# The last 69 adjacency visits inside the first aggregation, and a reordered context stretch

## Time and profile before

| | |
|---|---|
| time of the profiled execution | 481.68 us |
| its span, first to last instruction | 479.9 us |
| granted TensorE clock, mean | 0.992 |
| PE busy | 456.2 us (95%), 2517 matmuls |
| VectorE busy | 327.6 us (68%) |
| ScalarE, GpSimd busy | 154.1 us (32%), 66.2 us (14%) |
| 262 of the visits on TensorE (L749) | 35.9 us |
| their marks on VectorE (L1850, L1851) | 68.1 and 64.6 us |

### The profile page before, as it was taken

The page is one execution under the profiler, slowest core; times in us unless marked ns, Lnnn a source line. Parts: engine busy times, 40 slices in busy tenths (PEclk is TensorE's granted clock), DMA queues, the critical chain, the costliest instruction groups (busy, mean ns, idle before and its releaser), DMA issues.

```text
span 479.9 us, 7046 instructions
## 1 busy us (share of the span) xinstructions
PE 456.2 (95%) x2517; PEld 365.4 (76%) x2517; DVE 327.6 (68%) x1108; ACT 154.1 (32%) x282; POOL 66.2 (14%) x95
## 2 busy tenths in 40 slices
PE   8999996899999999989999999999999998978996
PEld 5777785678778786968887999987877775655784
DVE  6988597668887978789997011244655656778982
ACT  4665882204223142342123111121223123660110
POOL 5434600000000000000000400000500000006662
PEclk9999998989999999999999999999999999999999
DMA  8910200170000000020300000000754439604892
GB/s 266 264 48 2 88 0 1 19 197 21 2 1 0 2 0 2 2 87 2 122 2 0 5 0 1 1 1 0 259 156 133 136 121 325 221 2 140 283 378 80
DMA packets 20415, 40.46 MB, mean 84 GB/s; under 512 B 2521, under 2 KB 2851, under 8 KB 20373
## 3 DMA queue, kind: packets, MB, share of 16 engines
q1 hardware_dynamic: 18117, 32.53, 21.6%
q0 software_dynamic: 2256, 7.39, 4.4%
HBM read 30.09 MB, written 10.31 MB: 84 GB/s over the span
## 4 chain that ended last, share of the span: by engine, by line
PE 71%; DVE 20%; ACT 4%; issue 3%; DMA 1%; POOLq 0%; POOL 0%; SPq 0%; DVEq 0%
PE ps L762 27%; PE ps L1104 9%; PE ps L1026 9%; PE ps L945 6%; PE ps L749 4%; PE ps L963 3%; DVE RING_D L1850 2%; DVE RING_S L1851 2%; PE ps L804 2%; ACT scrap_a L1529 1%; PE ps L890 1%; DVE QTL L1783 1%; DVE ESUM L1770 1%; PE ps L1121 1%; ACT QTH L1259 1%
## 5 line engine op out<-in xcount | busy, mean ns | idle before, releaser
L1850 DVE TENSOR_SCALAR RING_D<-places,PLACES 125x170 bf16<-125x170 f16 (+1 forms) x262 | 68.1, 260 | 0.0
L1851 DVE TENSOR_SCALAR RING_S<-iota,HOME 125x128 bf16<-125x128 f16 x262 | 64.6, 246 | 0.0
L749 PE MATMUL ps<-RING_D,RING_S 125*125 125x170 bf16 (+1 forms) x262 | 35.9, 246 | 2.7
L1026 PE MATMUL ps<-AT,H1H 125*128 125x416 f32 (+1 forms) x108 | 38.0, 352 | 0.1
L1026 PE MATMUL ps<-AT,H1L 125*128 125x416 f32 (+1 forms) x108 | 38.0, 351 | 0.0
L749 PEld LDWEIGHTS ps<-RING_D,RING_S 125*125 125x125 bf16 x262 | 26.6, 136 | 14.6 <-DVE RING_S L1851 7.5
L1104 PE MATMUL ps<-H2H,AT 125*125 125x512 f32 x90 | 36.1, 402 | 0.0
L1121 PE MATMUL ps<-WE0H 128*128 128x512 f32 x129 | 35.5, 408 | 0.0
L1104 PE MATMUL ps<-H2L,AT 125*125 125x512 f32 x90 | 35.5, 394 | 0.0
L623 POOL TENSOR_TENSOR G2L<-RAW_G,G2H 128x512 fp32r<-128x512 f32 x4 | 5.0, 1292 | 205.5 <-ACT G2H L1259 205.5
L1998 DVE SCALAR_TENSOR_TENSOR ZL<-ps,ZH 128x416 fp32r<-128x416 f32 (+1 forms) x12 | 6.3, 585 | 39.1 <-ACT ZH L1471 39.1
(11 more groups left out here) (416 smaller groups left out, 1174.6 us busy)
## 6 DMA issues: line engine op xcount, KB each, us to landing
RAW_E<-in_experts SPq DMA_DIRECT2D x8, 1024.0 KB, 10.1
RAW_AGAIN<-in_experts SPq DMA_DIRECT2D x3, 1024.0 KB, 11.8
X<-in_x SPq DMA_DIRECT2D x1, 2240.0 KB
out_x<-X SPq DMA_DIRECT2D x10, 224.0 KB
scratch<-X SPq DMA_DIRECT2D x10, 224.0 KB
scratch<-Y SPq DMA_DIRECT2D x10, 224.0 KB
RAW<-in_mW2T SPq DMA_DIRECT2D x4, 256.0 KB, 4.2
RAW_A<-in_mW SPq DMA_DIRECT2D x4, 256.0 KB, 4.6
```

The lines of the kernel that those rows point to most:

```text
L749: pe.matmul(PS[4 + g % 2][0:TT, o:o + width(b)], hot_s(v)[:, 0:TT], hot_d(v, width(b)), start=(s == 0), stop=(s == VISITS[b] - 1), skip_gr ...
L1026: pe.matmul(place(f), h[0:TT, k, 128 * f:128 * (f + 1)], AT[0:TT, k, c0:c1], start=(k == 0 and n == 0), stop=False)
L1850: V.tensor_scalar(hot_d(v, width(b)), places[0:ET, 0:width(b)], PLACES[0:ET, c:c + 1], None, ALU.is_equal)
L1851: V.tensor_scalar(hot_s(v), iota[0:ET, :], HOME[0:ET, c:c + 1], None, ALU.is_equal).then_inc(done["marked"], 1)
```

## The change

- `Z_BANKS` gives the aggregation's units their banks: chunk 0 on 2, 3, 0, 1, chunk 1 on 6, 7, 2, 3, chunk 2 on 0, 1, 4, 5; before these were 0 to 3, 4 to 7, 0 to 3.
- `visits_in_products` has 69 visits fewer in the products before the aggregation (value products 4 to 2 a batch; most batches of the pairs two fewer; h0 to h8 7 or 6 to 5 or 4) and puts the last 69 (`LATE`), the last eight groups from group 17 on (`FIRST_LATE`), in the eight units of chunks 0 and 1: nine or eight a unit, in front of its eleventh matmul.
- TensorE decides on `flag` first. In the branch that is taken, each unit runs over all ten tiles at once, with its visits, and waits only for the groups that its chunk needs. Chunk 2 waits for all groups, and is as before. In the branch not taken, both chunks stand as well.
- VectorE marks the first late batch ahead of the bias of h8, then in each unit makes five marks, stores the unit's finished groups itself (`store_late`, ahead of it ScalarE's task), makes the rest, and takes ZL.
- In the context stretch query tile 1's turn passes bank 6 instead of 4; `round_q` and `q_left` stand two and one tile earlier; `add_exp` begins at tile 5 instead of 7 of the loop, and `chosen_keys` stands behind the sums.
- Behind it the first `total_left` stands first, ahead of the flag; the six marks that stood there go, and `mark_next(3)` stands behind the marks of "cp".

```diff
--- before.py
+++ after.py
@@ -62,6 +62,9 @@
 COLUMNS = [NE + 1, *range(NE), NE]
 LEFT_ORDER = [1, 0, *range(2, NE)]
 RING = 6
+FIRST_LATE = 17
+LATE = sum(VISITS[SIDE * FIRST_LATE:])
+Z_BANKS = ((2, 3, 0, 1), (6, 7, 2, 3), (0, 1, 4, 5))
 LANES = 16
 STEPS = [2040, 128, 8, 1, 4096, 256, 16, 2]
 ROUNDS = len(STEPS)
@@ -112,7 +115,7 @@
         use(f"tt{c}", low, ("th_ready", c + 1), ("tl_ready", c + 1))
     use("ranks", (5,), ("tiles_step", 3))
     for i in range(2):
-        use(f"qt{i}", (4,), ("qth_ready", i + 1), ("qtl_ready", i + 1))
+        use(f"qt{i}", (4 + 2 * i,), ("qth_ready", i + 1), ("qtl_ready", i + 1))
     use("homes", (6,), ("home_ready", 1))
     use("keys", (5,), ("place_key", 1))
     use("flag", (7,), ("flag_ready", 1))
@@ -137,7 +140,7 @@
     for ch in range(3):
         for f in range(C):
             n = ch * C + f + 1
-            use(f"z{ch}_{f}", (low, high, low)[ch], ("zh_ready", n), ("zl_ready", n))
+            use(f"z{ch}_{f}", (Z_BANKS[ch][f],), ("zh_ready", n), ("zl_ready", n))
     for i in range(NT):
         use(f"h2_{i}", high, ("h2h_ready", i + 1), ("h2l_ready", i + 1))
     for i in range(NT + 1):
@@ -196,18 +199,22 @@
 def visits_in_products():


-    spots = [("cp", n, 4) for n in range(12, 48, 6)]
+    spots = [("cp", n, 2) for n in range(12, 48, 6)]
     for p in range(PAIRS):
         a, b = 2 * p + 2, 2 * p + 3
         if a < NT:
-            spots += [(f"q{a}", 6, 9 if p else 5)]
-        spots += [(f"a{p}", 28, 10)]
+            spots += [(f"q{a}", 6, 7 if p else 5)]
+        spots += [(f"a{p}", 28, 8)]
         if b < NT:
-            spots += [(f"q{b}", 6, 9), (f"x{a - 2}", 6, 9), (f"x{b - 2}", 6, 10 if p else 9)]
+            spots += [(f"q{b}", 6, 7), (f"x{a - 2}", 6, 7), (f"x{b - 2}", 6, 8)]
         else:
-            spots += [(f"x{a - 2}", 0, 5), (f"x{a - 2}", 6, 5), (f"x{b - 2}", 6, 9)]
+            spots += [(f"x{a - 2}", 0, 4), (f"x{a - 2}", 6, 5), (f"x{b - 2}", 6, 9)]
     for i in range(NT - 1):
-        spots += [(f"h{i}", 6, 6 if i else 7)]
+        spots += [(f"h{i}", 6, 5 if i < 2 else 4)]
+    left = NV - LATE - sum(n for _, _, n in spots)
+    assert 0 <= left <= 4, left
+    spots = [(u, n, k + (u[0] == "h" and 2 <= int(u[1:]) < 2 + left)) for u, n, k in spots]
+    spots += [(f"z{ch}_{f}", 10, LATE // 8 + (C * ch + f < LATE % 8)) for ch in range(2) for f in range(C)]
     found, v = [], 0
     for unit, n, count in spots:
         found.append((unit, n, range(v, v + count)))
@@ -1005,40 +1012,61 @@
                       skip_group_check=True).then_inc(done["again_full"], 1)
         pe.wait_ge(done["again_go"], NG + 1)

-    pe.wait_ge(done["adj_hi"], NG)
+    def sources(ch, f, ks, visited=False):
+
+        c0, c1 = CHUNKS[ch]
+        for k in ks:
+            if ch == 0 and f == 0:
+                pe.wait_ge(done["h1l_ready"], k + 1)
+            for n, h in enumerate((H1H, H1L)):
+                if visited:
+                    visits(f"z{ch}_{f}", 2 * k + n)
+                mm = pe.matmul(PS[plan[f"z{ch}_{f}"][0]][:, 0:c1 - c0], h[0:TT, k, 128 * f:128 * (f + 1)], AT[0:TT, k, c0:c1],
+                               start=(k == 0 and n == 0), stop=(k == NT - 1 and n == 1))
+        if NT - 1 in ks:
+            closes(f"z{ch}_{f}", mm)
+
+    def more_counts(ch):
+
+        c0, c1 = CHUNKS[ch]
+        for k in range(NT):
+            pe.wait_ge(done["ac_ready"], ch * NT + k + 1)
+            for f in range(C):
+                for h in (H1H, H1L):
+                    mm = pe.matmul(PS[plan[f"z{ch}_{f}"][0]][:, 0:c1 - c0], h[0:TT, k, 128 * f:128 * (f + 1)], AC[0:TT, k % 2, 0:c1 - c0],
+                                   start=False, stop=False)
+            mm.then_inc(done["ac_used"], 1)
+
     pe.wait_ge(done["flag_ready"], 1)
     large.append(pe.value_load(flag[0:1, 0:1], min_val=0, max_val=1))
     with pe.If(large[0] > 0):
+        pe.wait_ge(done["adj_hi"], FIRST_LATE)
         count_again()
+        for ch in range(2):
+            for f in range(C):
+                opens(f"z{ch}_{f}")
+                sources(ch, f, range(NT - 1))
+            if ch == 0:
+                pe.wait_ge(done["h1l_ready"], NT)
+            more_counts(ch)
+            for f in range(C):
+                sources(ch, f, (NT - 1,))
+    with pe.Else():
+        for ch in range(2):
+            pe.wait_ge(done["adj_hi"], max(g + 1 for g in range(NG) if group(g)[0] < CHUNKS[ch][1]))
+            for f in range(C):
+                opens(f"z{ch}_{f}")
+                sources(ch, f, range(NT), visited=True)
+    pe.wait_ge(done["adj_hi"], NG)
+    for f in range(C):
+        opens(f"z2_{f}")
+        sources(2, f, range(NT - 1))
+    with pe.If(large[0] > 0):
+        more_counts(2)
     with pe.Else():
         pe.nop()
-
-    for ch, (c0, c1) in enumerate(CHUNKS):
-        def place(f):
-            return PS[plan[f"z{ch}_{f}"][0]][:, 0:c1 - c0]
-
-        for f in range(C):
-            opens(f"z{ch}_{f}")
-            for k in range(NT - 1):
-                if ch == 0 and f == 0:
-                    pe.wait_ge(done["h1l_ready"], k + 1)
-                for n, h in enumerate((H1H, H1L)):
-                    pe.matmul(place(f), h[0:TT, k, 128 * f:128 * (f + 1)], AT[0:TT, k, c0:c1], start=(k == 0 and n == 0), stop=False)
-        if ch == 0:
-            pe.wait_ge(done["h1l_ready"], NT)
-        with pe.If(large[0] > 0):
-            for k in range(NT):
-                pe.wait_ge(done["ac_ready"], ch * NT + k + 1)
-                for f in range(C):
-                    for h in (H1H, H1L):
-                        mm = pe.matmul(place(f), h[0:TT, k, 128 * f:128 * (f + 1)], AC[0:TT, k % 2, 0:c1 - c0], start=False, stop=False)
-                mm.then_inc(done["ac_used"], 1)
-        with pe.Else():
-            pe.nop()
-        for f in range(C):
-            k = NT - 1
-            pe.matmul(place(f), H1H[0:TT, k, 128 * f:128 * (f + 1)], AT[0:TT, k, c0:c1], start=False, stop=False)
-            closes(f"z{ch}_{f}", pe.matmul(place(f), H1L[0:TT, k, 128 * f:128 * (f + 1)], AT[0:TT, k, c0:c1], start=False, stop=True))
+    for f in range(C):
+        sources(2, f, (NT - 1,))

     pe.wait_ge(*lo_of("g2", C - 1))
     for i in range(NT):
@@ -1397,8 +1425,8 @@
             exp_q(i - 1)
         if i in (3, 4):
             scale_q(i - 3)
-        if i in (7, 8):
-            round_q(i - 7)
+        if i in (6, 7):
+            round_q(i - 6)
     reads(act, "homes")
     copy(HOME[0:ET, :], ps_of("homes")[0:ET, 0:NV]).then_inc(done["home_ready"], 1)
     act.wait_ge(done["esum_step"], NT)
@@ -1808,17 +1836,15 @@
             tiles_left()
         if C <= i < 2 * C:
             split_lo("wv", i - C)
-        if i >= 7:
-            add_exp(i - 7)
-        if i == 8:
-            q_left(0)
-        if i == 9:
-            q_left(1)
-    chosen_keys()
-    for i in range(3, NT - 2):
+        if i in (7, 8):
+            q_left(i - 7)
+        if i >= 5:
+            add_exp(i - 5)
+    for i in range(5, NT - 2):
         add_exp(i)
     add_exp(NT - 2)
     add_exp(NT - 1)
+    chosen_keys()
     def total_left(c):
         after("th_ready", c + 1)
         V.tensor_tensor(TL[:, c, :], ps_of(f"tt{c}")[:], TH[:, c, :].bitcast(F32), ALU.subtract).then_inc(done["tl_ready"], 1)
@@ -1866,13 +1892,14 @@
             dve.wait_ge(loads["x_again"], 16 * len(CUTS))
         V.tensor_tensor(X[0:TT, i, :], ps_of(f"xq{i}")[0:TT, :], X[0:TT, i, :], ALU.add).then_inc(done["mix_added"], 1)

-    mark_next(RING_A)
+    total_left(0)
     reads(dve, "flag")
     V.tensor_scalar(flag[0:1, 0:1], ps_of("flag")[0:1, 0:1], 0.5, None, ALU.is_gt).then_inc(done["flag_ready"], 1)
-    for c in range(C):
+    for c in range(1, C):
         total_left(c)
     value_scale()
     mark_to("cp")
+    mark_next(3)
     context_left(0)
     context_left(1)
     mark_to("q2")
@@ -1929,12 +1956,11 @@

     dve.wait_ge(loads["b1"], 16)
     for i in range(NT):
-        mark_to(f"h{min(i + 1, NT - 2)}")
+        mark_to(f"h{i + 1}" if i < NT - 2 else "z0_0")
         add_bias(1, i)
         if i:
             h1_left(i - 1)
     h1_left(NT - 1)
-    assert marked[0] == NV
     dve.wait_ge(loads["pairs"], 32)
     after("flag_ready", 1)
     large = dve.value_load(flag[0:1, 0:1], min_val=0, max_val=1)
@@ -1976,27 +2002,58 @@
             V.tensor_tensor(AL[0:TT, :, d], ps, AT[0:TT, :, d].bitcast(F32), ALU.subtract).then_inc(done["again_go"], 1)
         after("again_go", NG + 1)

+    def copy_residual(first, c0, c1):
+
+        for k in range(NT):
+            n = first + k
+            if n >= 2:
+                after("ac_used", n - 1)
+            V.tensor_copy(AC[0:TT, k % 2, 0:c1 - c0], AL[0:TT, k, c0:c1]).then_inc(done["ac_ready"], 1)
+
     def residual(first, c0, c1):

         with dve.If(large > 0):
-            for k in range(NT):
-                n = first + k
-                if n >= 2:
-                    after("ac_used", n - 1)
```

(44 more changed lines are left out.)

## The result

The changed kernel takes 471.92 us, the median of four runs (470.02 to 472.07), beside 482.85 for the kernel before in the same session (482.09 to 483.33). The ratio is 0.9766 [0.9738, 0.9794]. The forecast was 471.3, range 467.0 to 476.5.

The account below looks back on a forecast made before the run. TensorE, busy nearly all the time, was taken as the bound, with holes, low clock and batches waiting for marks. 10.0 + 10.0 - 5.5 - 0.2 - 3.0 = 11.3 us less, giving 471.3 us, range 467.0 to 476.5.

Parts of the forecast that it names:

- Part 1: Context stretch through value products: holes and low clock go, and visits leave the value products; 10.0 us less.
- a forecast of 5.55: Context stretch: last context group starts 5.55 us earlier, 3.78 from the hole before the second turn, the rest slow clock.
- The 2.0 of the next step: Before the value products: sums end before the context, first TL goes ahead of six marks; 2.0 us more gained.
- Part 2: Product stretch: 57 visits leave, saving 0.34 us each in mark-paced batches and 0.07 in others; 10.0 us less.
- Rival C: Product stretch: another wait replaces the paced ones, only 0.07 us a visit saved; 5.3 us less, 477.3; chance 0.1.
- Part 3: First aggregation: 5.5 us for 69 added visits, 0.2 for a later start, 3.0 of stall in the second unit.
- 0.6 for the jumps, of which GpSimd's time hides the most: Aggregation start: jumps over the long repeated-edges branch on VectorE and TensorE add 0.6 us to the stall.
- each of the four G2L can hold a mark, I take 4: Aggregation start: each GpSimd G2L holds a mark up to 1.26 us; 4 us taken, so marks end 2.4 late.
- rival D: Before the first aggregation: the branch jump costs far more, 14.6 us of stall; 0.3 us slower, 482.9; chance 0.05.
- rival A: Aggregation's second unit: no stall, marks slip past GpSimd and jumps are short; 14.3 us less, 468.3; chance 0.2.
- rival B: Aggregation becomes bound by VectorE: held marks, jump of some 3 us, never catching up; 7.3 less, 475.3; chance 0.15.
- the bounds (1.7): Aggregation's second unit: 1.7 us for a clock falling behind the stall, counted only in its upper bound of 7.

Follow-up runs that it names:

- e6: Changed kernel with query tile 1's turn put back on bank 4, so it waits for QTL of tile 0: 477.05 us.
- e7: Changed kernel with the sums begun at tile 7 of the loop again and the chosen keys ahead of the last seven: 472.88 us.
- e1: Kernel before with only the changed kernel's context stretch; all 291 visits stay where they were: 472.66 us.
- e10: Kernel before with the new context order and eight marks instead of four (five in the last pair) ahead of VectorE's waits; no visit moved: 464.13 us.
- e4: Changed kernel with VectorE's taken branch directly behind its decision and the rare one at the end; G2L stay: 472.04 us.
- e3: Changed kernel with GpSimd's four G2L held back until behind the second visited chunk: 470.47 us.
- e2: Changed kernel with the context stretch's order put back, so only the 69 visits are moved: 481.88 us.
- e5: Changed kernel with both VectorE's taken branch directly behind the decision and G2L behind the two visited chunks: 467.43 us.
- e8: Changed kernel with six marks instead of four (five in the last pair) ahead of VectorE's waits for TensorE in each pair: 465.17 us.
- e9: Changed kernel with more marks ahead of the waits, VectorE's taken branch directly behind the decision, and G2L behind the visited chunks: 461.06 us.

## Why the prediction was right or wrong

**Part 1 was right, step by step.** The second turn stands without a wait, the last context group starts at 82.33 (forecast 82.2), the value products at 88.71 (88.8) and end at 101.00 (101.1), at full clock. e6 gives the bank 5.1 us beside a forecast of 5.55. The 2.0 of the next step were for two things, sums that are no longer last and a first TL that no longer stands behind six marks. From the last context group on it measured 2.2 (8.60 to 6.38): e7, which puts back the sums alone, has 0.9 of it, so 1.3 is left for the place of TL, which no run puts back alone. e1 puts the whole at 9.6.

**Part 2 was right in size and in mechanism.** 10.1 us beside 10.0 in the profiled execution, a pair in 23.47 us beside 23.5, the residual stalls each within 0.1, and the 1.15 us for QTL at 195.60 stayed. Rival C (0.07 us a visit) would have left pairs at about 25. What the forecast did not ask is whether moving visits is the way to get this: e10 has it without moving one. The reading of the earlier trace rows, that the batches run at the pace of the marks, was the right one: e10 leaves their number and changes their order, and two of the three stalls all but go (0.69, 1.63 and 1.29 us become 0, 1.05 and 0.25). The further step is to look at what the marks are queued behind.

**Part 3: right sum, wrong parts.** 8.5 us beside 8.7, with a stall of 3.1 beside 3.0. But the step "0.6 for the jumps, of which GpSimd's time hides the most" failed. VectorE's jump costs 2.8 us (3.24 idle, and 0.47 without it in e4), and alone it makes a stall of 2.1 (e3). The step "each of the four G2L can hold a mark, I take 4" was right only where the jump is gone: e4 has four held operations and a stall of 2.7 beside the 2.4 forecast. In the changed kernel the jump covers most of the G2L and two operations are held, for 0.2 and 1.1 us. I took one of two causes too small, and the sum came out by luck, because they overlap. The repair that the forecast points at, G2L out of the way, is e3, and it gives 1.4 of the 4.5 us. TensorE's jump over its own rare branch shows nothing beside the 0.35 us for AT, which may cover a part of it, so rival D was off, and rival A would have needed both causes gone. Of rival B the jump of some 3 us came true, but not its end: steady units keep up with TensorE.

**Missed: the clock behind the stall.** The forecast had it in the bounds (1.7) and not in the sum. It measured 1.7 in e2, and by their mean clock it came in three of four executions of the changed kernel, so the median gain is 10.9 us while the profiled execution shows 11.7. The visits' part, forecast as 2.1 (10.0 + 0.8 - 5.5 - 0.2 - 3.0), is 0.4 by e2 and 1.3 by e1, neither told from nothing; that part 1 measured 9.6 in e1 beside the 9.2 that were forecast without visits makes up for some of it. That 471.9 lies so near to 471.3 is luck in part: a fall of the clock that was left out stands against parts that came out a little larger.

## What to carry to other kernels

A batch on the bounding engine that lasts longer than its fellows can be a wait that the idle column doesn't show, as here; before taking work out of it, look at what its producers are queued behind, and move them ahead of the waits. Where two things can cause one stall, price each with the other taken away, since each can hide the other, and removing one then shows little or nothing. Put the branch that is taken directly behind the decision, and keep work of GpSimd like these G2L away from the few microseconds in which VectorE's small operations are wanted. Only with both done did the stall go (e5).

## What the runs showed of the hardware

- VectorE's taken branch cost about 2.8 us: 2.79 to 3.11 us of issue time in the six kernels that have it at this place (2.79 in the kernel after and e2, 2.84 in e3 and e7, 3.09 in e8, 3.11 in e6), and nothing that shows where the target follows directly (e4, 0.47 us idle with the reading of the flag). The Trainium skill, "Runtime: NRT & Kernel Launch", section "Instruction fetch mechanics", says that a taken branch past the window of fetched instructions waits for a fetch; the trace fits this, and doesn't show the fetch to be the cause. These are prices for one distance, some 360 instructions. TensorE's branch, over some 330 by the same count, shows at most the 0.35 us in which it waits for AT.
- An operation of 0.26 us that begins inside a GpSimd operation of 1.26 us ends with it: 1.32, 1.34 us. In e4 the two engines took turns, one held operation of VectorE for each of the four G2L. The Trainium skill, "SBUF — State Buffer", section "SBUF: two separate sides", says that a VectorE operation in a two-port mode and a GpSimd operation exclude each other for a whole instruction, and the trace agrees; in which mode the marks run, it doesn't show. The row that the prediction went by (38.00, 1.16 us) is the other case of that section of the Trainium skill, an operation with two inputs in SBUF beside a GpSimd operation that reads SBUF; that marks are held was shown first by the kernel after and e4.
- Whether the clock falls behind the same partly filled stall of 3.1 us differs from one execution to the next: 470.02 us with a mean clock of 1.0, three others near 472.0 with 0.994 to 0.996. The mean clock doesn't account for every run: one of e4 takes 472.04 us at 1.0. In e5 and e9, without the stall, it is 0.998 or above.
